# GpSimd sends the results of two tiles, not of four, ahead of the second image's row stores

## What is computed

```python
x = _L0_conv_ref(x, ...)                        # group norm, 4-head attention over 1024 positions, residual
t = _to_tokens(x)                               # (2, 1024, 128)
t = t + _L1_attn_ref(_ln_t(t), ...)             # linear attention
t = t + _L1_ffn_ref(_ln_t(t), ...)
x = _from_tokens(t, x)

def _L1_ffn_ref(x, Wr, br, ln_g, ln_b, W1, b1, W2, b2):      # 8 experts, hidden size 512
    logits = xt @ Wr + br
    probs = jax.nn.softmax(logits, axis=-1)
    top_p, top_idx = jax.lax.top_k(probs, 2)
    weights = top_p / top_p.sum(axis=-1, keepdims=True)
    xn = (xt - mu) * jax.lax.rsqrt(var + LN_EPS)
    xe = xn[None, :, :] * ln_g[:, None, :] + ln_b[:, None, :]
    h = gelu(jnp.einsum('end,edh->enh', xe, W1) + b1[:, None, :])
    y = jnp.einsum('enh,ehd->end', h, W2) + b2[:, None, :]
    out = (weights[:, :, None] * sel).sum(axis=1)            # sel: the two chosen experts' y
```

## Time and profile before

| | us |
|---|---|
| median of 3 runs | 361.16 |
| lowest and highest of them | 359.86, 362.2 |
| the profiled execution, its own time | 362.47 |
| its span, from the first to the last instruction | 360.7 |
| TensorE busy | 315.8 (88%) |
| VectorE busy | 198.4 (55%) |
| ScalarE busy | 195.0 (54%) |
| GpSimd busy | 113.5 (31%) |

### The profile page before, as it was taken

The page is one execution under the profiler, slowest core; times in us unless marked ns, Lnnn a source line. Parts: engine busy times, 40 slices in busy tenths (PEclk is TensorE's granted clock), DMA queues, the critical chain, the costliest instruction groups (busy, mean ns, idle before and its releaser), DMA issues.

```text
span 360.7 us, 6258 instructions
## 1 busy us (share of the span) xinstructions
PE 315.8 (88%) x1885; PEld 196.0 (54%) x1885; DVE 198.4 (55%) x620; ACT 195.0 (54%) x305; POOL 113.5 (31%) x192
## 2 busy tenths in 40 slices
PE   7979899999999989999999798946580499999986
PEld 3533434344444434445432436746580399999985
DVE  1586435575757654564568537478540057776510
ACT  1370657677677745555576204672350187787722
POOL 2074193000000001000304771051277836556530
PEclk9996969999999999999999859996596599999999
DMA  6059886753000034000000113000011322224215
GB/s 196 4 120 207 185 188 269 191 180 122 0 2 3 3 106 129 0 2 1 2 0 24 45 37 74 8 9 8 9 52 59 103 61 69 75 72 120 92 42 222
DMA packets 20540, 27.88 MB, mean 77 GB/s; under 512 B 3831, under 2 KB 14508, under 8 KB 20252
## 3 DMA queue, kind: packets, MB, share of 16 engines
q1 hardware_dynamic: 15800, 17.57, 18.2%
q0 software_dynamic: 3520, 9.39, 8.3%
q10 hardware_dynamic: 1188, 0.53, 0.6%
HBM read 11.15 MB, written 8.33 MB: 54 GB/s over the span
## 4 chain that ended last, share of the span: by engine, by line
PE 71%; DVE 13%; POOL 5%; issue 4%; ACT 3%; DMA 2%; DVEq 1%; SPq 0%; POOLq 0%; ACTq 0%
PE ps L919 17%; PE ps L896 9%; PE ps L1160 8%; PE ps L1138 8%; PE ps L877 5%; PE ps L861 4%; POOL expert_in L530 4%; PE ps L756 2%; PE ps L955 2%; PE ps L828 2%; PE ps L796 2%; DVE pm L1275 1%; PE ps L946 1%; DMA Qs<-mrow 1%; PE ps L1117 1%
## 5 line engine op out<-in xcount | busy, mean ns | idle before, releaser
L598 ACT ACTIVATE probs<-ps 128x1024 f32<-128x1024 f32 x64 | 65.3, 1020 | 33.0 <-PE ps L896 32.9
L919 PE MATMUL ps<-probs,vT 128*32 128x512 f32 x256 | 69.4, 618 | 0.6 <-ACT probs L598 0.5
L919 PE MATMUL ps<-probs,ones 128*32 128x512 f32 x256 | 69.4, 618 | 0.0
L466 POOL TENSOR_TENSOR rstd<-ve,minus_half 128x8 f32<-128x8 f32 (+1 forms) x8 | 11.0, 1384 | 143.9 <-DVE ve L1326 76.4
L1272 DVE CUSTOM_DVE_ANT_0 above<-ps,above 128x512 f32<-128x512 f32 x56 | 38.7, 691 | 31.6 <-PE ps L877 29.8
L1138 PE MATMUL ps<-w,GT 128*128 x312 | 44.8, 290 | 9.0 <-ACT GT L734 9.0
L536 POOL DMA_INDIRECT token_out<-Y,yidx x39 | 37.7, 966 | 45.3 <-DVE Y L1606 43.0
L1618 DVE TENSOR_TENSOR H<-ps,b1T 128x512 f32<-128x512 f32 x39 | 27.0, 692 | 35.8 <-PE ps L1160 33.2
L1138 PEld LDWEIGHTS ps<-w,GT 128*128 128x128 f32 x312 | 40.6, 203 | 10.4 <-issue 10.3
L1160 PE MATMUL ps<-XTT,w1s 128*128 128x128 f32 x312 | 45.4, 293 | 0.2 <-ACT XTT L712 0.2
L896 PE MATMUL ps<-Qs,Ks 98*128 98x512 f32 x128 | 44.1, 426 | 1.2 <-issue 0.7
(11 more groups left out here) (233 smaller groups left out, 437.5 us busy)
## 6 DMA issues: line engine op xcount, KB each, us to landing
XR<-expert_in SPq DMA_DIRECT2D x39, 65.0 KB
Qs<-q_hi SPq DMA_DIRECT2D x16, 128.0 KB, 3.1
w<-in_L_ffn_W SPq DMA_DIRECT2D x1, 2048.0 KB, 8.4
w<-in_L_ffn_W SPq DMA_DIRECT2D x8, 256.0 KB, 4.3
YG<-token_out SPq DMA_DIRECT2D x8, 256.0 KB, 3.8
Ks<-k_hi SPq DMA_DIRECT2D x14, 128.0 KB, 2.4
expert_in<-zeros POOLq DMA_DIRECT2D x1, 1300.0 KB, 5.7
expert_in<-zeros POOLq DMA_DIRECT2D x1, 1235.0 KB, 8.1
```

The costliest lines, as they stand in the source:

```text
L598: nc.scalar.activation(probs[:, s % 3, :], bank(2 + 2 * (s % 2), 2), ACT.Exp).then_inc(exp_done, 1)
L919: last = nc.tensor.matmul(bank(value_bank(o))[i * HD:(i + 1) * HD, :], w, probs[:, s % 3, hd * HALF:(hd + 1) * HALF], start=kt == 0, stop= ...
```

## The change

`SENT_FIRST` goes from 4 to 2. GpSimd sends the results of tiles 0 and 1 ahead of the second image's row stores, as before, and those of tiles 2 and 3 behind them.

```diff
     NBY = 16
-    SENT_FIRST = 4
+    SENT_FIRST = 2
     GATES_AT = 14
```

## The result

| | before | after |
|---|---|---|
| median of 5 runs, us | 361.16 | 349.28 |
| after : before, 95% interval | | 0.968 (0.9635 to 0.9724) |
| the profiled execution, its own time | 362.47 | 353.42 |
| its span | 360.7 | 351.7 |

The kernel is 3.2% faster; 350.4 us, 0.970, were forecast. The interval taken to the median of before is 348.0 to 351.2 us, so forecast and measurement agree.

What follows compares the result with a forecast made beforehand. TensorE idles 14.47 us for tile 9, behind row stores held by the send of tile 2. 362.47 - 10.86 + 0.1 = 351.7 us, or 350.4 on the median's level; range 348.0 to 354.5.

Steps and rivals of the forecast that it cites:

- step 1: GpSimd, second image: with two sends no longer ahead, the first row store starts at 250.58 instead of 261.44, 10.86 us earlier.
- step 2: GpSimd's 16 row stores, now partly beside VectorE's tables, stay 1.26 us apart; the overlap costs 0.1 us, at most 4.05.
- the prediction's own sign: Named beforehand as showing the overlap estimate wrong: stores of over 0.96 us or larger gaps while VectorE is at the tables.
- this rival: The row stores wait for VectorE's second-image tables by the port rule: 354.4 us, 4.0 over the forecast; chance 0.10.
- step 3: TensorE gets tile 9 at 273.87 instead of 284.63, 10.76 us earlier, and waits 3.7 us instead of 14.47.
- the cover: TensorE's remaining 3.7 us gap ahead of tile 9: making tiles 3 to 8 later by up to that costs nothing.
- step 4: VectorE's tables and tiles 2 to 8 beside the stores, 250.6 to 270.6: a few tenths slower, inside the gap, cost 0.
- the slower rival: Stores hold VectorE back and tile 8's end becomes the bound: 362.1 us, or 368.8 with the sends; chance 0.04.
- step 5: Seven GpSimd sends behind the stores, 1.41 us apart, end at 280.4, about when tile 9's result is written; cost 0.
- step 6: TensorE's clock still falls in the gap before tile 9, with the same slow restart, cost 0; if held, 2.3 us more gain.

Runs made afterwards that it cites:

- the two kernels with ScalarE copies: The kernel after with four or twelve extra copies on ScalarE ahead of tile 8's weight copy: 351.27 and 354.13 us, 0.9738 and 0.9798 of the kernel before.

## Why the prediction was right

**The wait (step 1).** Right: the row stores stood behind the wait for the result of tile 2, and without it the slots release them. The size of the start was off: from the end of the slots to the first store 0.29 us, not the 0.75 that the sends showed, so 0.46 us earlier than forecast. It was 0.28 in the kernels with one send ahead and with the stores behind the tables too. I had taken a send for a store; why the store starts sooner, no run here shows.

**The stores beside the tables (step 2).** By the prediction's own sign (stores of over 0.96 us) this step was wrong. The mechanism was named and its price was too low: 0.67 us on the first and 0.24 on the third store, 0.91 in all, where 0.1 was taken from the first image's stores and 4.05 was the bound. The first image's tables have 72 columns where these have 720, so that the row that I took as nearest came from far shorter operations (0.23 us for line 1510 there, 0.91 here). The forecast and this rival aren't two cases: somewhat over a fifth of the rival's bound happened.

**Tile 9 (step 3).** Slots to tile 9 went down by 10.42 us, forecast 10.76: the two errors above, +0.46 and -0.81, make the difference. That they have opposite signs, so that the forecast is off by only 0.34 us, is luck.

**VectorE and the cover (step 4).** Right. `H` of tiles 3 to 8 stayed at 0.69 us, tile 8 ended ahead of tile 9's load, and the two kernels with ScalarE copies show the cover and its end. The cast of 0.40 us on which the slower rival leaned took 0.17 in the kernel after, beside the same send, so that the send alone did not make it long (VectorE's timeline):

```profile
247.67 0.17 DVE L1482 CAST cnt<-cnt_i 128x8 f32<-128x8 int32 x1
```

**The sends that moved (step 5).** Right: 1.41 us apart, done at 281.9, the result of tile 9 didn't wait for GpSimd; with one send ahead even a longer backlog cost nothing.

**The clock (step 6).** Right in the profiled executions of the kernel after: gaps of 3.97, 5.47 and 3.89 us, and a product of 2.07 or 2.08 us behind each. The moment of the fall was less sure than the 2.4 us of the one row that I had: it came 3.0, 1.4 and 3.0 us behind the last product of tile 8 in these three. A clock that holds gave 1.5 to 1.9 us, where the prediction put 2.3 on it.

## What to carry to other kernels

On an engine that works through its list in order, look at what a wait holds up behind it: here the send of tile 2, started at 257.19, was needed only when tile 18's result took over its buffer, at 308.29 in the kernel before, and stood ahead of stores for which TensorE waited 14.5 us. The gain of moving it ends where the next releaser stands, which can be read from the trace before the change (the slots at 249.83), and a further move gives nothing. When work comes to lie beside another engine's, price the overlap with operations of the same length and the same operands, not merely of the same name.

## What the runs showed of the hardware

An indirect transfer that GpSimd issues and that begins within a VectorE operation with two SBUF operands can be held by it. Of the second image's row stores that began within line 1510 or 1523 (numbered as in the kernel after), in the kernel after and its variants, 15 were held and ended 0.83 or 0.84 us behind the operation; they began 0.04 to 0.43 us behind its start. Six were not held and kept 0.96 us: three that began 0.04 or 0.05 us behind the start, beside which the operation took 0.48 instead of 0.41 us, and three that began in the operation's last 0.06 us. Beside a sum with one operand, or `H` with one operand in PSUM, a store keeps its 0.96 us.

Executions of one kernel differ by some microseconds through the clock in a place that the change doesn't touch. The four products of line 955 (eight instructions), timeline of TensorE in the kernel after and in its next run:

```profile
207.05 7.19 PE L955 MATMUL ps<-bqv,ones 1*128 1x512 f32 x8
```

```profile
207.11 3.98 PE L955 MATMUL ps<-bqv,ones 1*128 1x512 f32 x8
```

In a third profiled execution of the same kernel they took 7.19 us again, and the slots ended at 249.68, against 248.10 with 3.98 us. The granted clock from 203.3 to 213.0 was 0.58 in that execution and 0.87 in the faster one. All twelve profiles fall into these two groups: four with 7.19 us, among them the kernel before and the kernel after, with the slots' end at 249.68 to 250.95, and eight with 3.8 to 4.3 us, with it at 247.64 to 248.23. Before comparing two profiles it pays to cut them at events that both have, as above, and to compare only the stretch that the change touches.
